# A gated attention and mixture-of-experts kernel: attention and expert 0 in two halves of the tokens, a chain each, and the inverse deviation as GpSimd's power

## The chip, the cores and the metric

One core of a Trainium2 chip. The metric is the device time of one execution in microseconds. TensorE's clock has two levels here, 1.2 and 2.4 GHz, which the profile shows as a granted clock of 0.50 and 1.00.

## The reference, cut to what matters

Sixteen sequences of 56 tokens with 128 features: 896 tokens. First an attention by autocorrelation over the time shifts, with a gate, then a mixture of eight experts, with a gate. Everything is float32.

```python
x = x + tanh(g_xattn) * xattn(layernorm(x), ctx, ctx)
x = x + tanh(g_ffn) * ffn(layernorm(x))

def xattn(query, key, value):                 # 16 heads of 8 features
    Q, K, V = query @ Wq + bq, key @ Wk + bk, value @ Wv + bv     # ctx cut to 56 tokens
    corr = irfft(rfft(Q) * conj(rfft(K)))     # along the tokens
    w, idx = top_k(corr.mean(features), 4)    # of the 56 shifts, for each head
    w = softmax(w)
    out = sum_k w[k] * roll(V, idx[k])
    return out @ Wo + bo

def ffn(x):                                   # 8 experts, 128 -> 512 -> 128
    logits = x @ Wr + br
    weights = softmax(logits, all but the top two masked out)
    h = gelu(x @ W1[e] + b1[e])
    return sum_e (h @ W2[e] + b2[e]) * weights[:, e]
```

## The kernel before, in words

**Layout.** The tokens are 8 tiles of 112 (two sequences each, `NT`, `PT`), in two halves of 4 tiles (`HT`). Half a set of spectra is `HS` = 464 columns, half the tokens `TOK` = 448 columns. The five engines have a queue each, written out by hand, each in the order of the program; they meet at semaphores. PSUM is one tensor `bank` of eight banks, and each step has its bank.

**Attention.** TensorE turns context and normalised input into spectra (L658), projects them to keys, values and queries (`project_spectra`, L664; a bias opens each at L648). ScalarE takes the projected spectra (`take`, L357 to L364); VectorE multiplies queries by keys (L496) and adds the products (L261). TensorE sums per head (L691) and turns back to correlations (L698). VectorE finds the four largest shifts and their weights (L519 to L535), TensorE transposes these (L710) and takes their spectra (L714), VectorE puts them into the columns that own them (`wown`, L543), TensorE repeats them over the rows (L724), VectorE multiplies them with the values (L496) and adds (L261), TensorE makes the output products (L730) and turns them back into tokens (L735) on top of the residual (L718). Each step is done for both halves before the next step begins, on every engine.

**Normalising** (`normalise` of VectorE, L459 to L485): four or eight statistics (L457), eight aggregations (L463), a variance with epsilon (L465), and a guess with two Newton steps for its inverse root, ten dependent small instructions from L465 to L476, each waiting for the one before; then the shift (L478) and the tiles, some by VectorE (L484), some by ScalarE (L354). All eight tiles together, once for the input and once for the attended tokens.

**Fillers.** `keep_busy` (L639) issues products of zeros of 512 columns on TensorE, which nobody reads: 13 at the start, 4 ahead of the transposed weights, 2 ahead of their spectra, 8 ahead of the transposed normalised tokens (L644, L707, L711, L751).

**Experts.** Float32 by three products of a rounded lead and its rest: `weh`, `wel` for the weights, `xth`, `xtl` for the tokens, `hidh`, `hidl` for the hidden values. An expert has four chunks of 128 hidden features; a chunk `n` (0 to 31) is `hidden(n)` (L772, six products of 448 columns: three operand pairs by two halves), ScalarE's Gelu (L409) and lead (L416), VectorE's rest (L617), and `project(n)` (L799, six products). TensorE's order is `hidden(n + 2)`, `project(n)`. Chunks 0 and 31 are split into halves at Gelu, lead and rest. The routing (L568 to L589 on VectorE, a tanh on ScalarE at L431) runs in VectorE's queue behind the rests of chunks 0 and 2; `turn_routes` (L780) stands in TensorE's queue before `project(3)`, and the turned routes go to DRAM and back, spread over the partitions (L283, L290).

**Taking an expert.** VectorE multiplies an expert's sum with its routes into `scaled` (`take_expert`, L604; expert 0 into `acc`), which lies over `kf` and `cf` in the rows; GpSimd adds `scaled` to `acc` (L329), and VectorE may take the next expert only after that, since there is one `scaled` for each half:

```python
if e >= 2:
    ve.wait_ge(acc_ok, 2 * (e - 2) + half + 1)
```

The takes of expert 2 stand behind the rests of chunks 13 and 14 in VectorE's queue (the table `takes`, L610), those of expert 0 behind chunks 7 and 8.

**GpSimd's queue** (L299 to L337): `centre`, the residual with the output bias (`xres`, L308), then for each of the eight experts its weights' rest (`wel`, L323), for experts 2 to 7 the lead too (`weh`, L321; ScalarE does those of experts 0 and 1 at L376), and only behind all eight the additions of L329, for expert 1 with the attended tokens (L333). At the end it does 160 of the last 448 columns (L337). The experts' weights come through a ring of three slots; a load waits until the expert three before is split (L276). SP issues experts 0 to 6, then waits for the routes.

Of the kernel before, what the change touches and what calls it, by code (L numbers as in the profile page):

```python
# [10 lines left out]
I32 = mybir.dt.int32  # L29
# [16 lines left out]
FILL_START, FILL_TOP, FILL_STEP, FILL_NORM = 13, 4, 2, 8  # L46
# [11 lines left out]
GUESS = float(0x5F1FFFF9)  # L58
STEP_A, STEP_B = 0.703952253, 0.703952253 * 2.38924456
# [44 lines left out]
def build(nc, x, tab_ctx, w_attn, bias_rows, gates, shared_rows, cols, w_experts, tab_b, out, route_dram):  # L104
    with ExitStack() as stack:
# [22 lines left out]
        xres = sb("xres", [PT, NT, D])  # L128
        stat = sb("stat", [PT, NT, 6])
        mv = sb("mv", [PT, NT, 2])  # L130
        var = sb("var", [PT, NT])
        rs_a = sb("rs_a", [PT, NT])
        rs_b = sb("rs_b", [PT, NT])
        rs_c = sb("rs_c", [PT, NT])
        rs_d = sb("rs_d", [PT, NT])
# [64 lines left out]
        dve = sem("dve_done")  # L200
        c_spec, cf_ok = sem("context_spectra"), sem("context_spectra_in_sbuf")
        norm_ok, xn_v, xn_s = sem("norm_factors"), sem("xn_by_vector"), sem("xn_by_scalar")
        x_spec, xf_ok = sem("x_spectra"), [sem("x_spectra_in_sbuf0"), sem("x_spectra_in_sbuf1")]
        k_proj, v_proj, q_proj = sem("k_projected"), sem("v_projected"), sem("q_projected")
        k_ok, v_ok = sem("k_in_sbuf"), sem("v_in_sbuf")
        qk_mul, heads, rsb_ok = sem("queries_times_keys"), sem("head_sums"), sem("head_sums_in_sbuf")
        corr, ntop_ok, cexp_ok = sem("correlations"), sem("top_found"), sem("correlation_exponentials")
        wraw_ok, wt_mm, wt_ok = sem("shift_weights"), sem("shift_weights_transposed"), sem("shift_weights_t_in_sbuf")
        ws_mm, wown_ok, warm_ok = sem("weight_spectra"), sem("weight_spectra_in_their_columns"), sem("filler_cleared")
        dc_ok = sem("length_in_row")  # L210
        wrep, of_mul = sem("weight_spectra_repeated"), sem("weights_times_values")
        qk_ok = [sem(f"cross_spectra{half}") for half in range(2)]
        of_ok = [sem(f"output_spectra{half}") for half in range(2)]
        stat_ok = sem("statistics")
# [7 lines left out]
        lead_s, lead_p, we_split, pool = sem("weights_lead_by_scalar"), sem("weights_lead_by_pool"), sem("weights_split"), sem("pool_done")  # L222
# [3 lines left out]
        last_half, sum_v, sum_p = sem("last_expert_half"), sem("sum_complete_by_vector"), sem("sum_complete_by_pool")  # L226
        stored = sem("stored")

        BY_SCALAR = ((3, 6, 7), (3, 6))
        LEAD_BY_SCALAR = 2  # L230

# [6 lines left out]
        CUT = 288  # L238

        def norm_counts(n, times):  # L240

            before = sum(len(tiles) for tiles in BY_SCALAR[:times])
            if n in BY_SCALAR[times]:
                return xn_s, before + BY_SCALAR[times].index(n) + 1
            return xn_v, times * NT - before + [i for i in range(NT) if i not in BY_SCALAR[times]].index(n) + 1

        IN_HALVES = (0, E * HC - 1)

        def parts(n):

            return [(0, slice(0, 1)), (1, slice(1, 2))] if n in IN_HALVES else [(0, slice(0, 2))]

        def upto(n, part=None):

            last = len(parts(n)) if part is None else part + 1
            return n + (1 if n > 0 else 0) + last
# [9 lines left out]
        def _(sp):  # L266
# [3 lines left out]
            sp.dma_start(rows_sb[:, :, :], bias_rows).then_inc(in_rows, 16)  # L270
# [3 lines left out]
            def load_expert(e):  # L274
                if e >= RING:
                    sp.wait_ge(we_split, 2 * (e - RING + 1))  # L276
# [8 lines left out]
            for e in range(E):  # L285
                if e == ROUTES:
                    load_expert(E - 1)
                if e >= ROUTES:
                    sp.wait_ge(scaled_ok, 2 * (e - ROUTES + 1))
                sp.dma_start(route_b[:, e % ROUTES, :, :], route_dram[e:e + 1].broadcast_to([D, 2, TOK])).then_inc(in_route[e], 16)  # L290
            for half in range(2):
                sp.wait_ge(sum_v, half + 1)
                if half == 1:
                    sp.wait_ge(sum_p, 1)
                sp.dma_start(out[:, half, :], o_sb[:, half, :]).then_inc(stored, 16)
# [3 lines left out]
        def _(gp):  # L299
            by_vector = [NT - len(tiles) for tiles in BY_SCALAR]  # L300
            gp.wait_ge(in_tb, 16)
            gp.wait_ge(xn_v, by_vector[0])
            gp.tensor_scalar(centre[:, :], ident, 1.0 / D, None, ALU.subtract).then_inc(centre_ok, 1)
# [4 lines left out]
            gp.tensor_tensor(xres[:, :, :], x_sb[:, :, :], shared[:, 0:D].unsqueeze(1).broadcast_to([PT, NT, D]),  # L308
                             ALU.add).then_inc(xres_ok, 1)

            for e in range(E):
                gp.wait_ge(in_we[e], 16)
                if e == 0:
                    gp.wait_ge(of_ok[0], 1)
                if e == 1:
                    gp.wait_ge(xn_v, sum(by_vector))
                for k in range(2):
                    if e < LEAD_BY_SCALAR:
                        gp.wait_ge(lead_s, 2 * e + k + 1)
                    else:  # L320
                        gp.tensor_copy(weh[:, e, k, :], we_sb[:, e % RING, k, :]).then_inc(lead_p, 1)  # L321
                        gp.wait_ge(lead_p, 2 * (e - LEAD_BY_SCALAR) + k + 1)
# [12 lines left out]
            gp.wait_ge(scaled_ok, 2 * E)  # L335
# [517 lines left out]
```

## Time and profile before

| | us |
|---|---|
| median of 3 runs | 133.5 (132.34 to 134.25) |
| the profiled execution | 132.46 |
| its span, first to last instruction | 130.2 |
| TensorE busy | 117.5 (90%) |
| VectorE busy | 89.9 (69%) |
| ScalarE busy | 80.5 (62%) |
| GpSimd busy | 62.9 (48%) |
| mean granted clock of TensorE | 0.956 |

The profile comes from one execution; its own time is 132.46 us, and the 2.26 us between that and the span lie outside the first and last instruction. "Busy" counts instructions at work, waits excluded; a float32 product on TensorE is several passes, so busy doesn't mean at its peak. L12 is line 12 of the kernel before. PE is TensorE's products, PEld its weight loads, DVE VectorE, ACT ScalarE, POOL GpSimd, SP SyncE.

### The profile page before, as it was taken

To read this page: it belongs to the slowest core of one execution; us is meant where nothing else is said; L and a number is where in the kernel's file an instruction comes from. 1 tells how busy PE (TensorE), PEld (TensorE's weight loads), DVE (VectorE), ACT (ScalarE), POOL (GpSimd) and SP (SyncE) were. 2 spreads that over 40 slices of the span, in tenths; PEclk is the share of its full clock that TensorE was granted. 3 is DMA by queue.
4 is the path that set the end of the run, shared out by engine and by line. 5 is a ranking of instruction groups with operands and counts; after the bars stand their busy time and mean duration, and the time that the engine had idled before them with its cause. 6 is when DMAs were issued, how large, how long until landed. Compare 5 with 4: busy or idle time off the path is not lost.

```text
span 130.2 us, 1685 instructions
## 1 busy us (share of the span) xinstructions
PE 117.5 (90%) x575; PEld 94.7 (73%) x575; DVE 89.9 (69%) x175; ACT 80.5 (62%) x107; POOL 62.9 (48%) x50
## 2 busy tenths in 40 slices
PE   6999969998878993959999999999999999999950
PEld 2397555544465891939999999999999999999930
DVE  1583687529386498999679877775775775775991
ACT  3027764401355755928878878878878878878900
POOL 0001460005203999999999999980330330330802
PEclk9999995559999999999999999999999999999998
DMA  3896000000310215400891340030040030000003
GB/s 93 234 406 249 0 0 5 3 0 0 101 60 0 82 79 161 162 6 9 238 337 43 107 146 0 0 141 0 0 141 3 5 141 0 0 0 0 0 0 141
DMA packets 3833, 10.07 MB, mean 77 GB/s; under 512 B 697, under 2 KB 1066, under 8 KB 3826
## 3 DMA queue, kind: packets, MB, share of 16 engines
q1 hardware_dynamic: 3154, 9.43, 21.5%
q10 hardware_dynamic: 672, 0.55, 1.5%
q8 instruction: 4, 0.07, 0.2%
q14 instruction: 3, 0.02, 0.1%
HBM read 9.49 MB, written 0.49 MB: 77 GB/s over the span
## 4 chain that ended last, share of the span: by engine, by line
PE 70%; DVE 14%; ACT 5%; issue 5%; POOL 2%; POOLq 1%; DVEq 0%
PE bank L772 23%; PE bank L799 22%; PE bank L641 7%; PE bank L658 3%; ACT prod L409 3%; POOL cf L329 2%; DVE hidl L617 2%; PE bank L664 2%; ACT hidh L416 2%; DVE prod L496 2%; DVE tw L496 2%; PE bank L718 2%; PE bank L735 1%; DVE qk L261 1%; PE bank L748 1%
## 5 line engine op out<-in xcount | busy, mean ns | idle before, releaser
L617 DVE TENSOR_TENSOR hidl<-prod,hidh 128x896 fp32r<-128x896 f32 (+1 forms) x34 | 45.3, 1339 | 19.8 <-ACT hidh L416 19.8
L409 ACT ACTIVATE prod<-bank,col_sb 128x896 f32<-128x896 f32 (+1 forms) x34 | 32.9, 967 | 14.5 <-PE bank L772 11.8
L323 POOL TENSOR_TENSOR wel<-we_sb,weh 128x512 fp32r<-128x512 f32 x16 | 25.6, 1604 | 20.9 <-issue 19.9
L416 ACT CAST hidh<-prod 128x896 fp32r<-128x896 f32 (+1 forms) x34 | 30.5, 899 | 1.0
L329 POOL TENSOR_TENSOR cf<-cf,kf 128x448 f32<-128x448 f32 x12 | 17.9, 1496 | 26.6 <-DVE kf L604 26.4
L799 PE MATMUL bank<-hidl,weh 128*128 128x448 f32 x64 | 18.5, 368 | 2.2 <-DVE hidl L617 2.2
L772 PE MATMUL bank<-xth,weh 128*128 128x448 f32 x64 | 18.6, 366 | 0.3 <-ACT xth L404 0.3
L772 PE MATMUL bank<-xtl,weh 128*128 128x448 f32 x64 | 18.6, 367 | 0.0
L772 PE MATMUL bank<-xth,wel 128*128 128x448 f32 x64 | 18.5, 365 | 0.0
L799 PE MATMUL bank<-hidh,weh 128*128 128x448 f32 x64 | 18.4, 367 | 0.0
L799 PE MATMUL bank<-hidh,wel 128*128 128x448 f32 x64 | 18.3, 365 | 0.0
L799 PEld LDWEIGHTS bank<-hidl,weh 128*128 128x128 f32 x64 | 11.9, 188 | 3.8 <-DVE hidl L617 2.8
L772 PEld LDWEIGHTS bank<-xth,weh 128*128 128x128 f32 x64 | 12.0, 188 | 1.4 <-issue 0.5
L772 PEld LDWEIGHTS bank<-xtl,weh 128*128 128x128 f32 x64 | 12.0, 188 | 1.3 <-DVE xtl L562 0.3
L799 PEld LDWEIGHTS bank<-hidh,wel 128*128 128x128 f32 x64 | 12.0, 188 | 1.0
L772 PEld LDWEIGHTS bank<-xth,wel 128*128 128x128 f32 x64 | 12.0, 188 | 0.9
L799 PEld LDWEIGHTS bank<-hidh,weh 128*128 128x128 f32 x64 | 11.9, 188 | 0.9
L321 POOL CAST weh<-we_sb 128x512 fp32r<-128x512 f32 x12 | 12.2, 1017 | 0.0
L641 PE MATMUL bank<-filler 128*128 128x512 bf16 x27 | 10.2, 540 | 1.2 <-DVE filler L451 1.2
L604 DVE SCALAR_TENSOR_TENSOR kf<-bank,col_sb,route_b 128x448 f32<-128x448 f32 x14 | 9.4, 676 | 0.0
L641 PEld LDWEIGHTS bank<-filler 128*128 128x128 bf16 x27 | 3.5, 139 | 5.6 <-issue 3.6
L392 ACT ACTIVATE y_sb<-bank,tanh_g 116x512 f32<-116x512 f32 x2 | 1.4, 690 | 8.6 <-PE bank L730 8.6
(118 smaller groups left out, 116.7 us busy)
## 6 DMA issues: line engine op xcount, KB each, us to landing
we_sb<-in_w_experts SPq DMA_DIRECT2D x8, 512.0 KB, 5.0
route_b<-route_scratch SPq DMA_DIRECT2D x8, 448.0 KB, 3.6
out<-vf SPq DMA_DIRECT2D x2, 224.0 KB, 1.9
tb<-in_tab_b SPq DMA_DIRECT2D x1, 297.0 KB, 6.3
ta_c<-in_tab_ctx SPq DMA_DIRECT2D x1, 274.8 KB, 4.9
wa_sb<-in_w_attn SPq DMA_DIRECT2D x1, 256.0 KB, 5.7
x_sb<-in_x SPq DMA_DIRECT2D x1, 224.0 KB, 3.8
x_sb<-in_x ACTq DMA_DIRECT2D x1, 224.0 KB, 4.1
```

The source lines that it names most:

```text
L321: gp.tensor_copy(weh[:, e, k, :], we_sb[:, e % RING, k, :]).then_inc(lead_p, 1)
L323: gp.tensor_tensor(wel[:, e, k, :], we_sb[:, e % RING, k, :], weh[:, e, k, :].bitcast(F32), ALU.subtract).then_inc(we_split, 1)
L329: gp.tensor_tensor(acc[:, half, :], acc[:, half, :], scaled[:, half, :], ALU.add).then_inc(acc_ok, 1)
L409: act.activation(hid[:, n % 2, halves, :], bank[:, 2 * (n % 2):2 * (n % 2) + 2, 0:TOK][:, halves, :], ACT.Gelu, bias=col_sb[:, P_B1 + n:P_ ...
L416: act.copy(hidh[:, n % SLOTS, halves, :], hid[:, n % 2, halves, :]).then_inc(hid_hi, 1)
L496: return ve.tensor_tensor(products, a.unsqueeze(1).broadcast_to([D, kinds, HS]), pair, ALU.mult).then_inc(multiplied, 1)
L604: ve.scalar_tensor_tensor(out=into[:, half, :], in0=bank[:, 6 - 2 * (e % 2) + half, 0:TOK], scalar=col_sb[:, P_B2 + e:P_B2 + e + 1], in1=r ...
L617: ve.tensor_tensor(hidl[:, n % SLOTS, halves, :], hid[:, n % 2, halves, :], hidh[:, n % SLOTS, halves, :].bitcast(F32), ALU.subtract).then ...
L641: pe.matmul(bank[:, into, :], filler[:, 0:D], filler[:, :], start=True, stop=True)
L658: return pe.matmul(bank[:, first + i // HT, (i % HT) * PS:(i % HT + 1) * PS], src[:, i, :], ta[:, A_FWD:A_FWD + PS], start=(i % HT == 0), ...
L772: mm = pe.matmul(bank[:, 2 * slot + half, 0:TOK], w[:, e, 0, cols_], t[:, half, :], start=(k == 0), stop=(k == 2))
L799: mm = pe.matmul(bank[:, 6 - 2 * (e % 2) + half, 0:TOK], w_of(operands[k][0]), operands[k][1][:, slot, half, :], start=(c == 0 and k == 0) ...
```

## The change

- **Two chains.** Every step of attention becomes a function of one half, and each engine's queue is written anew with the first half ahead. Values of a half are projected between head sums and correlations.
- **Inverse deviation.** The Newton steps go. VectorE makes a half's variances, GpSimd raises them to the power -0.5 (`invert`), VectorE goes on with the shift.
- **Expert 0 in halves.** Chunks 0 to 3 run half by half (`HALF[0]`, `HALF[1]`), the first half's chunks ahead, chunks 4 to 30 on both halves as before, 31 in halves.
- **Fillers.** 7 and 5 at the start; none later.
- **GpSimd.** Its queue starts with the load of the bias rows. The rests of experts 0 and 1 are made in pieces of 128 columns and no longer wait for attention's steps. Behind both inversions of the second normalising it waits for the routes (`route_ok`), and then splits experts 2 to 7. The additions stay behind the splits. The last half's sum is all VectorE's.
- **SP.** Experts 0 to 4 are loaded ahead of the routes, 5 to 7 between the loads of the spread routes.
- **ScalarE.** The tanh of the gates comes first; it copies both halves' x spectra and the turned shift weights, which were VectorE's in part.

```diff
-FILL_START, FILL_TOP, FILL_STEP, FILL_NORM = 13, 4, 2, 8
+FILL_FIRST, FILL_SECOND = 7, 5
...
-        BY_SCALAR = ((3, 6, 7), (3, 6))
+        BY_VECTOR = (2, 3)
         LEAD_BY_SCALAR = 2
+        PIECE = 128
...
-            for e in range(E - 1):
+            for e in range(RING + LEAD_BY_SCALAR):
                 load_expert(e)
             sp.wait_ge(route_sb, 2)
...
+                if e >= 1 and e + RING + LEAD_BY_SCALAR - 1 < E:
+                    load_expert(e + RING + LEAD_BY_SCALAR - 1)
...
         def _(gp):
+            gp.dma_start(rows_sb[:, :, :], bias_rows).then_inc(in_rows, 16)
+            gp.memset(minus_half[:, :], -0.5).then_inc(half_ok, 1)
...
+            def invert(times, half):
+                tiles = slice(half * HT, (half + 1) * HT)
+                gp.wait_ge(var_ok, 2 * times + half + 1)
+                gp.tensor_tensor(rstd[:, tiles], var[:, tiles], minus_half[:, :], ALU.pow).then_inc(rstd_ok, 1)
...
+            for e in range(LEAD_BY_SCALAR):
+                gp.wait_ge(in_we[e], 16)
+                for k in range(2):
+                    gp.wait_ge(lead_s, 2 * e + k + 1)
+                    rest(e, k)
+            invert(1, 0)
+            invert(1, 1)
+            gp.wait_ge(route_ok, 1)
+            for e in range(LEAD_BY_SCALAR, E):
+                gp.wait_ge(in_we[e], 16)
+                for k in range(2):
+                    gp.tensor_copy(weh[:, e, k, :], we_sb[:, e % RING, k, :]).then_inc(lead_p, 1)
...
         @block.vector
...
+            variances(0, 0)
...
+            normalise(x_sb, 0, 0)
+            normalise(x_sb, 0, 1)
+            scores(0)
+            scores(1)
+            head_sums(0)
+            shift_weights(0)
+            head_sums(1)
+            weight_sum(0)
+            own_columns(0)
+            shift_weights(1)
+            weight_sum(1)
+            weighted(0)
+            output_spectra(0)
+            own_columns(1)
+            weighted(1)
+            ve.wait_ge(attn, 1)
+            moments(tiled(bank[0:PT, 0, :]), 0)
+            output_spectra(1)
+            variances(1, 0)
+            normalise(x2, 1, 0)
...
+            rest_of_hidden(1, HALF[1])
+            chosen()
+            rest_of_hidden(2, HALF[1])
+            routes()
+            rest_of_hidden(3, HALF[1])
...
         @block.tensor
...
+            head_sums(0)
+            values(0)
+            correlations(0)
+            head_sums(1)
+            weights_turned(0)
+            correlations(1)
+            weight_spectra(0)
+            values(1)
+            repeated(0)
+            weights_turned(1)
+            add_residual(0)
+            weight_spectra(1)
+            output_products(0)
+            repeated(1)
+            attention(0)
+            add_residual(1)
+            centred_router()
+            output_products(1)
+            attended_turned(0)
+            attention(1)
+            tokens_turned(0)
+            logits(0)
+            attended_turned(1)
+            hidden(0, HALF[0])
+            hidden(1, HALF[0])
+            logits(1)
+            hidden(2, HALF[0])
+            project(0, HALF[0])
+            tokens_turned(1)
+            hidden(3, HALF[0])
+            project(1, HALF[0])
+            hidden(0, HALF[1])
+            project(2, HALF[0])
...
+            hidden(4, BOTH)
+            project(2, HALF[1])
+            turn_routes()
+            hidden(5, BOTH)
+            project(3, HALF[1])
```

## Rows read from the trace of the kernel before

**Rows 1.** The page: TensorE's clock in forty slices of 3.26 us, in tenths.

```profile
PEclk9999995559999999999999999999999999999998
```

**Rows 2.** Stretches: length, busy (instructions) by engine, granted clock, DMA share, GB/s.

```profile
25.00:30.00 5.00, 5.00 (x8) 2.15 (x8) 2.40 (x4) 0.00 (x0) 0.00 (x0) 0.51 0.00 0
...
42.00:58.60 16.60, 12.63 (x63) 10.73 (x64) 13.86 (x28) 10.26 (x15) 16.12 (x15) 1.00 0.29 96
58.60:116.90 58.30, 58.30 (x289) 54.02 (x288) 42.37 (x39) 46.98 (x48) 34.83 (x24) 1.00 0.22 73
```

**Rows 3.** The chain that ended last: start, length, what.

```profile
25.13 1.98 PE bank L718 x2
27.11 1.56 PE bank L724 x2
...
33.58 1.90 PE bank L735 x4
...
42.15 1.05 PE bank L772 x3
...
58.55 1.23 PE bank L799 x6
```

**Rows 4.** Timeline of VectorE and GpSimd in attention: start, length, instruction.

```profile
14.21 1.12 DVE L496 TENSOR_TENSOR prod<-bank,kf 128x928 f32<-128x928 f32 x1 [2.32 <-PE bank L664]
...
14.69 0.61 POOL L306 TENSOR_SCALAR shared<-shared,tanh_g 112x128 f32<-112x128 f32 x1 [3.60 <-ACT tanh_g L373]
...
15.37 0.64 DVE L261 TENSOR_TENSOR qk<-prod 128x464 f32<-128x464 f32 x1
15.39 2.85 POOL L308 TENSOR_TENSOR xres<-x_sb,shared 112x1024 f32<-112x1024 f32 x1
...
34.47 1.92 DVE L457 BATCH_NORM_STATS2 stat<-bank 112x6 f32<-112x128 f32 x8 [2.08 <-PE bank L735]
...
37.17 0.17 DVE L465 TENSOR_SCALAR var<-mv 112x8 f32<-112x8 f32 x1
...
39.20 0.17 DVE L478 SCALAR_TENSOR_TENSOR shift<-mv,rstd 112x8 f32<-112x8 f32 x1
```

**Rows 5.** Stretches of half a microsecond, columns as in rows 2.

```profile
18.00:18.50 0.50, 0.00 (x0) 0.00 (x0) 0.50 (x1) 0.32 (x2) 0.23 (x1) 1.00 0.00 0
...
19.50:20.00 0.50, 0.50 (x11) 0.38 (x10) 0.19 (x1) 0.00 (x0) 0.00 (x0) 0.67 0.00 0
...
30.00:30.50 0.50, 0.50 (x3) 0.14 (x1) 0.50 (x2) 0.00 (x0) 0.00 (x0) 1.00 0.00 0
```

**Rows 6.** Timeline of ScalarE: chunk 0 in halves.

```profile
43.22 1.24 ACT L409 ACTIVATE prod<-bank,col_sb 128x448 f32<-128x448 f32 x2 [0.78 <-PE bank L772]
44.36 1.02 ACT L416 CAST hidh<-prod 128x448 fp32r<-128x448 f32 x2
```

**Rows 7.** Timeline of GpSimd from 43 to 80 us.

```profile
43.52 0.61 POOL L321 CAST weh<-we_sb 128x512 fp32r<-128x512 f32 x1
...
48.72 1.28 POOL L323 TENSOR_TENSOR wel<-we_sb,weh 128x512 fp32r<-128x512 f32 x1
...
57.43 1.61 POOL L321 CAST weh<-we_sb 128x512 fp32r<-128x512 f32 x1
...
76.19 2.01 POOL L329 TENSOR_TENSOR cf<-cf,kf 128x448 f32<-128x448 f32 x1
...
91.57 1.16 POOL L329 TENSOR_TENSOR cf<-cf,kf 128x448 f32<-128x448 f32 x1 [4.14 <-DVE kf L604]
```

**Rows 8.** Timeline of VectorE: the route weights, and the taking of expert 2.

```profile
56.75 0.82 DVE L589 SCALAR_TENSOR_TENSOR route<-lexp,tanh_g,linv 112x64 f32<-112x64 f32 x1
...
80.09 1.09 DVE L617 TENSOR_TENSOR hidl<-prod,hidh 128x896 fp32r<-128x896 f32 x1 [0.94 <-ACT hidh L416]
81.09 0.68 DVE L604 SCALAR_TENSOR_TENSOR kf<-bank,col_sb,route_b 128x448 f32<-128x448 f32 x1
82.51 1.94 DVE L617 TENSOR_TENSOR hidl<-prod,hidh 128x896 fp32r<-128x896 f32 x1 [0.74 <-ACT hidh L416]
```

More of the change, by code:

```diff
@@ L236, in tiled, with normalised, unit, split @@
             return t.rearrange("p (i d) -> p i d", d=D)
[L238 to L256, printed above, removed]
+        def normalised(i, times):
+            half, j = i // HT, i % HT
+            if j < BY_VECTOR[times]:
+                return xn_v, times * 2 * BY_VECTOR[0] + half * BY_VECTOR[times] + j + 1
+            by_scalar = [HT - n for n in BY_VECTOR]
+            return xn_s, times * 2 * by_scalar[0] + half * by_scalar[times] + j - BY_VECTOR[times] + 1
+        def unit(n, half):
+            if n < HC:
+                return n + 1 + HC * half
+            return n + HC + 1 + (half if n == LAST else 0)
+        SPLITS = [2 * (H // PIECE if e < LEAD_BY_SCALAR else 1) for e in range(E)]
+        def split(experts):
+            return sum(SPLITS[:experts])
+        BOTH = slice(0, 2)
+        HALF = (slice(0, 1), slice(1, 2))
         def add_products(engine, products, out_, done):
@@ L433, in _ @@
+            chunk(2, HALF[1])
+            chunk(3, HALF[1])
+            for n in range(HC, LAST):
+                chunk(n, BOTH)
+            chunk(LAST, HALF[0])
+            chunk(LAST, HALF[1])
         @block.vector
@@ L508, in _, with head_sums @@
+            def head_sums(half):
                 ve.wait_ge(heads, half + 1)
@@ L546, in _, with weighted @@
                                         op0=ALU.mult, op1=ALU.mult).then_inc(wown_ok, 1)
-            for half in range(2):
+            def weighted(half):
                 ve.wait_ge(wrep, half + 1)
@@ L693, in _, with correlations @@
                 mm.then_inc(heads, 1)
-            for t in range(2):
+            def correlations(t):
                 pe.wait_ge(rsb_ok, t + 1)
@@ L732, in _, with attention @@
                 mm.then_inc(y_mm, 1)
-            for half in range(2):
+            def attention(half):
                 pe.wait_ge(y_ok, half + 1)
@@ L761, in hidden, with tokens_turned @@
+            def tokens_turned(half):
+                pe.wait_ge(wrc_ok, 1)
+                for i in range(half * HT, (half + 1) * HT):
+                    pe.wait_ge(*normalised(i, 1))
+                    mm = pe.transpose(bank[:, 6 + half, (i % HT) * PT:(i % HT + 1) * PT], xn[:, i, :], ident[0:PT, 0:PT])
+                mm.then_inc(xt_mm, 1)
+            def hidden(n, halves):
+                e, c, slot, last = n // HC, n % HC, n % 2, halves.stop - 1
                 if c == 0:
-                    pe.wait_ge(we_split, 2 * e + 1)
+                    pe.wait_ge(we_split, split(e) + SPLITS[e] // 2)
```

563 lines of the change are left out of this document (280 added, 283 removed).

## The prediction

> **What bounds the kernel now.** I read the totals and the forty slices of the page first. TensorE is busy 117.5 of 130.2 us, and its clock line stands at 5 tenths in the seventh to ninth slice [rows 1]. Next the stretches: from 58.6 to 116.9 TensorE is busy all 58.30 us at the full level (2.4 GHz), with VectorE at 42.37 and ScalarE at 46.98. Between 42.0 and 58.6 it works 12.63 of 16.6 us. Between 25 and 30 it is busy throughout, but at a granted clock of 0.51 (1.2 GHz) [rows 2]. So 24 chunks of an expert (twelve products each) take 58.3 us, 2.43 each, and all 32 need 77.8 us. The change can't shorten that; it can only start it earlier and lose less in it. The chain of waits gives the marks of today: the shift weights' spectra are repeated over the rows from 27.11 to 28.67, the second attention product ends at 35.48, the first expert product starts at 42.15, and chunk 3, the last of expert 0, ends at 58.55+1.23=59.8 [rows 3].
>
> **1. Scores to repeated weights.** Before the scores little changes: the statistics still run beside the context spectra, and the Newton steps taken out there save nothing as long as GpSimd's power needs under about 1 us. Following the queues I have half 0 normalised at 8.4, its spectra taken at 10.4, its queries projected at 12.1 and its keys taken at 12.95. Its product (1.12) and sum (0.64) then begin at 13.0 instead of 14.21 [rows 4]. One half now needs: product and sum 1.8, head sums and correlations 1.6, shift weights 1.2 (both halves take 1.9 now), turn and spectrum 0.9, own columns 0.65. In between stand, on VectorE, the second half's scores (to 17.1) and, on TensorE, the first half's values and later the second's. I get correlations(0) at 17.9, shift weights(0) at 19.2, own columns at 21.3, values(1) done at 22.7, repetition(0) from 22.75 to 24.3: 4.35 us earlier than now, with TensorE at the low level as it is now.
>
> **2. The clock.** TensorE stands still from 18.0 to 18.5 at 1.00; in 19.5 to 20.0 the granted clock is 0.67, a mixture of the two levels, and half of full speed behind it. It is back at 1.00 in 30.0 to 30.5 [rows 5], after the five busy microseconds of [rows 2]. The change keeps the narrow products and the waits of that place, takes six fillers away and puts two value products of 464 columns between. I take fall and rise where they are now. Then residual(0) 1.98 [rows 3], weight spectrum(1) 0.5, output products(0) 1.3 and repetition(1) 1.56 end at 30.1, attention(0) at full level at 31.0 (two take 1.90 [rows 3]), and VectorE, which weights the second half until 31.3, ends the first statistics (half of 1.92 [rows 4]) at 32.3. If the level never fell, each of the low products would take half and this would be near 28.5.
>
> **3. Attention to the first expert product.** Behind those statistics come the output sum 0.64, aggregation and variance 0.55, the power, the shift 0.2, three tiles at 0.27; TensorE then does attention(1), turned tokens and logits, ScalarE the lead of 0.49. The power isn't in this trace. GpSimd's nearest rows run from 0.61 us for 128 columns to 2.85 for 1024 [rows 4]; for four numbers a partition I take 0.5, nearest to the short one; below lies at most 0.4 more, since something must be handed over. With the handing over it replaces nine of the ten steps from 37.17 to 39.20 [rows 4], 1.8 us, by 0.7. The eight fillers of 1.7 us ahead of the turned tokens go as well. The first product comes 5.4 us behind statistics(0), at 37.7 instead of 42.15: 4.5 earlier (33.9, or 8.2 earlier, if the level stays up).
>
> **4. Expert 0 in halves.** A half chunk costs TensorE 1.21 and ScalarE 0.62+0.51=1.13 [rows 6]; ScalarE has 1.3 us more for a tile, the second half's lead and a tanh. Following both queues I find no gap over 0.7 us: eight half chunks 9.7, chunks 4 and 5 hidden 2.4, logits(1) and the second turn 1.3, the turned routes 0.9, gaps 0.8, so 15.1 us to the end of chunk 3 against 17.6 now (59.8-42.15). Chunk 3 ends at 52.8 instead of 59.8: **7.0 us** earlier. SP's new order costs nothing: expert 5 is asked for when expert 2 is split, two experts of GpSimd's pace ahead of its own turn, and the later ones likewise.
>
> **5. What the wait for the routes costs.** Here the gain goes. GpSimd splits experts 2 to 7, twelve pairs of a cast and a difference. Only behind them in its queue stands the first addition, and that frees the one buffer into which VectorE takes expert 2. Now the pairs begin at 43.52 and the addition runs from 76.19 to 78.20 [rows 7]; VectorE asks at 81.09 [rows 8], with 2.9 us to spare. Changed, they begin with the route weights. From those to VectorE's request are 23.5 us now (57.57 to 81.09 [rows 8]) and by the order of chunks 24.0 then. How many pairs fit? One alone is 0.61+1.28=1.9; the six from 57.43 to 76.19 [rows 7], beside this same VectorE work, took 18.76, 3.1 each, the later ones 2.8. So 6+5.2/2.8=7.9 pairs are done. The 4.1 that are left go at 1.9, since VectorE stands still, 7.8 us, and the addition takes 1.16: VectorE waits **9.0 us** in chunk 13. The bounds: at 2.3 (the six pairs from 43.52 to 57.43) 10.4 pairs are done and the wait is 4.2; at 3.1 throughout it is 9.2.
> The Trainium skill's "GPSIMD Engine Reference", section 1 (Specifications), says that GpSimd contends with VectorE instructions that have two SBUF inputs. If these excluded it wholly, ten of them at 1.09 would leave 13.1 us, 6.9 pairs and a wait of 10.9. The rows agree in direction (1.09 against 1.94 for the same instruction [rows 8]) and show less than exclusion, so the sum goes by them.
> TensorE has work in hand: the rest of chunk 14 would end 1.8 us behind the request, and isn't due before 86.1 on today's times, so 3.2 us are absorbed. TensorE stands for 5.8, and 0.2 more a chunk later. After so long a stand it may come back at the low level. The price is half the time until it rises; the low stretch of now is 10.3 us (19.7 to 30.0), dense work should end it sooner. I take 1.5, with 0 and 5 as ends. Together 7.5.
>
> **6. The end.** The last sum is VectorE's alone, 0.63 instead of 0.46 beside GpSimd's 0.79, which decides now: -0.2.
>
> **Sum.** -7.0+7.5-0.2=+0.3 on this execution's 132.46 us (span 130.2 and 2.26 around it): 132.8. The median of the three runs, 133.5, lies 1.0 above it. I state 132.5.
>
> **Rivals.**
> *A, the forecast*: the gain is made and GpSimd's late start takes it back. 132.5; own range 129.5 to 135.5. For it speak the queue's order and [rows 7].
> *B, less is taken back*: pairs at 2.3, a wait of 4.2, TensorE stands 1.2 with the end of it, no low level: 132.46-7.0+1.2-0.2=126.5; if the level stays up in attention too, 3.7 less: 122.8. For it: GpSimd's rate before 57 us; against it: the rate after.
> *C, slower*: TensorE is at the low level when the experts start, since eight fillers went and only narrow products and waits lie between statistics(0) and the first one. Half chunks cost 2.4 instead of 1.2 until it rises; ten such microseconds lose 5: 132.5+5=137.5. It decides at the first expert product, 0.4 us each instead of 0.2. Against it: the clock line is at 9 in every slice from 30 us on [rows 1], gaps included.
> *D, slower*: the power is long. At 2.85 us the first costs 1.8 (1 us has cover) and that of half 0 behind attention 2.3: 136.6. The point is a power above 1.5 us.
> The same "GPSIMD Engine Reference", section 2.1 (Instruction dispatch), states some 6 us of loading at the first call of a freshly loaded function. Paid once at the start, 5 of it without cover, it would give 137.5. No row here shows one.
>
> **Chances.** A 0.42, B 0.31, C 0.17, D 0.10. Two per cent, about what a measurement of this kernel can tell from no change, are 130.8 and 136.2. Faster: nearly all of B and a fifth of A, 0.38. Slower: most of C, half of D, a little of A, 0.20. Same 0.42. The range 126 to 137 leaves out the low part of B and the high one of C.
>
> **What would show it.** Right: first expert product near 37.7; chunk 3 ending near 53; GpSimd's first cast at the route weights; VectorE's take of expert 2 waiting some 9 us for GpSimd's addition, and a hole of 6 us in TensorE in chunks 14 to 16. Wrong: pairs near 2 us and no hole (B); granted clock 0.5 inside expert 0 (C); power rows over 1.5 us (D). If the clock is 1.00 from 19.5 to 30, step 2 was wrong and 3.7 us more come off.

## The result, and the profile after

The changed kernel takes 135.24 us (median of 20 runs, 133.15 to 137.0) against 133.61 for the kernel before (20 runs, 130.57 to 134.89), with a ratio of 1.019 and a 95% interval of 1.013 to 1.026. Every ratio here compares the means of those executions alone that lie within 1.5% of the fastest of their kernel (9 of the 20 against 5 of the 20; the quotient of the two medians is 1.012), and the profiles of no_route_wait, before_with_route_wait and before_wait_additions come from executions above that, so that only their stretches and waits are read. So the changed kernel is slower, by 1.9% by the ratio. The forecast was 132.5 us in a range of 126 to 137, so the time lies in the range, but on the other side of the kernel before than the forecast did. The profiled execution took 134.32 us with a span of 132.5.

First the page, as in [rows 1]: TensorE's busy time and granted clock in slices of 3.31 us.

```profile
PE   6399997999789999999999990199999999999960
...
PEclk9977998569999999999999999658999999999998
```

Three things are new. TensorE is idle for most of the second slice and its clock drops in the third and fourth, before the scores of attention. The low stretch of attention is shorter. And in the middle of the experts stands a hole of two slices, with low clock in it and behind it. The same in stretches, with the columns of [rows 2]:

```profile
42.00:58.60 16.60, 16.60 (x89) 15.00 (x88) 12.70 (x31) 14.70 (x23) 7.91 (x6) 1.00 0.21 61
58.60:116.90 58.30, 52.31 (x246) 47.53 (x245) 37.20 (x33) 39.50 (x41) 38.29 (x31) 0.94 0.22 74
...
79.70:85.70 6.00, 0.04 (x1) 0.00 (x0) 2.48 (x2) 0.00 (x0) 5.34 (x6) 0.82 0.00 1
85.70:90.40 4.70, 4.67 (x13) 4.17 (x14) 3.62 (x3) 3.19 (x4) 4.48 (x4) 0.50 0.26 98
```

From 42.0 to 58.6, where TensorE worked 12.63 us before [rows 2], it works all 16.60. From 58.6 to 116.9, where it never paused, it now loses 6.0 us, and in 79.7 to 85.7 only GpSimd and, at the end, VectorE work. The marks that answer to [rows 3], from the timeline of TensorE: first expert product, last product of chunk 3, last products ahead of the hole (the time in which TensorE stands still), first behind it.

```profile
38.80 0.45 PE L839 MATMUL bank<-xth,weh 128*128 128x448 f32 x1
...
53.03 0.37 PE L864 MATMUL bank<-hidl,weh 128*128 128x448 f32 x1
...
79.17 0.57 PE L864 MATMUL bank<-hidh,wel 128*128 128x448 f32 x2
85.73 1.12 PE L864 MATMUL bank<-hidl,weh 128*128 128x448 f32 x2 [5.99 <-DVE hidl L583]
```

The first expert product is at 38.80 instead of 42.15 and chunk 3 is over at 53.4 instead of 59.8, 6.4 us ahead. Then TensorE waits 5.99 us for the rest of a hidden chunk, and that is VectorE's. VectorE's timeline says why it is late, and GpSimd's says what it waits for; they answer to [rows 8] and [rows 7].

```profile
50.10 0.28 DVE L616 SCALAR_TENSOR_TENSOR route<-lexp,tanh_g,linv 112x64 f32<-112x64 f32 x1
...
73.69 1.43 DVE L583 TENSOR_TENSOR hidl<-prod,hidh 128x896 fp32r<-128x896 f32 x1 [1.23 <-ACT hidh L410]
83.19 0.68 DVE L627 SCALAR_TENSOR_TENSOR kf<-bank,col_sb,route_b 128x448 f32<-128x448 f32 x1 [8.07 <-POOL cf L326]
83.79 1.88 DVE L583 TENSOR_TENSOR hidl<-prod,hidh 128x896 fp32r<-128x896 f32 x1
```

```profile
50.45 0.93 POOL L318 CAST weh<-we_sb 128x512 fp32r<-128x512 f32 x1 [10.99 <-DVE route L616]
...
80.76 1.26 POOL L320 TENSOR_TENSOR wel<-we_sb,weh 128x512 fp32r<-128x512 f32 x1
81.98 1.12 POOL L326 TENSOR_TENSOR cf<-cf,kf 128x448 f32<-128x448 f32 x1
```

Behind the rest of chunk 13 (ready at 75.1) VectorE is to take expert 2; it starts at 83.19, after 8.07 us, released by GpSimd's addition of 81.98. That addition stands behind twelve pairs of cast and difference, and the first of these has itself waited 10.99 us for the route weights. The chain of waits goes through GpSimd's pairs from 50.45 to 82 without a gap; on the page GpSimd has 26% of the chain that ended last, against 2% before.

### The profile page after: what moved, and what is told of

Read it like the earlier page. It is cut to its first block, busy times and chain, and to the rows that moved or that the text cites. A ratio compares the mean times of both kernels' runs of the same rounds, so it can differ in the third digit from the quotient of the medians.

```text
span 132.5 us, 1688 instructions
## 1 busy us (share of the span) xinstructions
PE 116.3 (88%) x560; PEld 95.6 (72%) x560; DVE 82.8 (62%) x163; ACT 82.9 (63%) x117; POOL 65.7 (50%) x68
## 4 chain that ended last, share of the span: by engine, by line
PE 48%; POOL 26%; ACT 9%; DVE 7%; DMA 4%; issue 3%; DVEq 0%; POOLq 0%
PE bank L864 17%; PE bank L839 15%; POOL wel L320 14%; POOL weh L318 9%; DMA rows_sb<-in_bias_rows 4%; PE bank L710 3%; ACT prod L402 3%; PE bank L731 2%; ACT hidh L410 2%; PE bank L773 2%; PE bank L787 2%; POOL cf L326 1%; PE bank L706 1%; PE bank L780 1%; PE bank L702 1%
## 5 line engine op out<-in xcount | busy, mean ns | idle before, releaser
L583 DVE TENSOR_TENSOR hidl<-prod,hidh 128x896 fp32r<-128x896 f32 (+1 forms) x37 | 46.3, 1257 | 18.2 <-ACT hidh L410 18.2
L326 POOL TENSOR_TENSOR cf<-cf,kf 128x448 f32<-128x448 f32 x12 | 16.9, 1415 | 24.6 <-DVE kf L627 24.5
L864 PE MATMUL bank<-hidl,weh 128*128 128x448 f32 x64 | 19.8, 378 | 6.0 <-DVE hidl L583 6.0
L839 PE MATMUL bank<-xth,weh 128*128 128x448 f32 x64 | 19.8, 378 | 0.0
L864 PE MATMUL bank<-hidh,weh 128*128 128x448 f32 x64 | 19.5, 374 | 0.0
L864 PE MATMUL bank<-hidh,wel 128*128 128x448 f32 x64 | 19.4, 373 | 0.0
L320 POOL TENSOR_TENSOR wel<-we_sb,weh 128x512 fp32r<-128x512 f32 x12 | 18.4, 1532 | 1.0
L282 POOL TENSOR_TENSOR rstd<-var,minus_half 112x4 f32<-112x4 f32 x4 | 4.2, 1047 | 15.3 <-DVE var L496 15.3
L287 POOL TENSOR_TENSOR wel<-we_sb,weh 128x128 fp32r<-128x128 f32 x16 | 7.1, 476 | 6.4 <-ACT weh L370 6.4
L513 DVE TENSOR_TENSOR prod<-bank,kf 128x928 f32<-128x928 f32 x2 | 2.2, 1124 | 6.8 <-ACT kf L365 6.8
```

The source lines that it names most:

```text
L282: gp.tensor_tensor(rstd[:, tiles], var[:, tiles], minus_half[:, :], ALU.pow).then_inc(rstd_ok, 1)
L287: gp.tensor_tensor(wel[:, e, k, at:at + PIECE], we_sb[:, e % RING, k, at:at + PIECE], weh[:, e, k, at:at + PIECE].bitcast(F32), ALU.subtra ...
L320: gp.tensor_tensor(wel[:, e, k, :], we_sb[:, e % RING, k, :], weh[:, e, k, :].bitcast(F32), ALU.subtract).then_inc(we_split, 1)
L326: gp.tensor_tensor(acc[:, half, :], acc[:, half, :], scaled[:, half, :], ALU.add).then_inc(acc_ok, 1)
L583: ve.tensor_tensor(hidl[:, n % SLOTS, halves, :], hid[:, n % 2, halves, :], hidh[:, n % SLOTS, halves, :].bitcast(F32), ALU.subtract).then ...
L839: mm = pe.matmul(bank[:, 2 * slot + half, 0:TOK], w[:, e, 0, cols_], t[:, half, :], start=(k == 0), stop=(k == 2))
```

## The experiments

**1. Without GpSimd's wait for the routes** (no_route_wait).

```diff
-            gp.wait_ge(route_ok, 1)
             for e in range(LEAD_BY_SCALAR, E):
```

> The changed kernel with one wait less: GpSimd no longer waits for the route weights before it splits experts 2 to 7. Theory 'late start': the splits begin at 39.5 instead of 50.45, right behind the last power, and end some 10 us earlier, near 72; VectorE's 8.1 us wait in chunk 13 and TensorE's hole of 6.0 us go, and with them the 4.7 us at the low level and the slower steps behind it. The routing chain and the halves' rests run beside GpSimd again and lose up to 1.5. Time 135.2-9+1=127 (ratio to before 0.95). Rival 'pace': the splits are slowed by the contention as much as they gain by the start, or the hole has another cause; then it stays within 2 us of 135 (ratio near 1.01).

Measured: 133.85 us, ratio 1.005 (0.998 to 1.011). The expectation missed by 7 us: the hole went to under 2 us (waits of 1.14 and 0.56), but the time hardly moved. Two things took its place. In the routing stage TensorE lost what it had gained, from the profile of this kernel:

```profile
42.00:52.00 10.00, 6.94 (x38) 5.51 (x37) 9.90 (x21) 6.57 (x13) 9.68 (x9) 1.00 0.00 1
```

where the changed kernel works 10.00 of the same 10 us. VectorE is busy 9.90 of them, and TensorE's longest wait there (2.31 us) is for it: it has become the bound. From the first expert product to the end of chunk 3 it takes 19.7 us instead of 14.6. And GpSimd, now early, stood still:

```profile
67.88 0.61 POOL L317 CAST weh<-we_sb 128x512 fp32r<-128x512 f32 x1 [12.88 <-DMA we_sb<-in_w_experts]
...
84.34 1.16 POOL L325 TENSOR_TENSOR cf<-cf,kf 128x448 f32<-128x448 f32 x1
```

It waited 12.88 us for expert 5, whose load stands in SP's queue behind the trip of the routes (asked for at 61.88), so its first addition was at 84.34, no earlier than with the wait. With the wait in place that order of the loads had cost nothing.

**2. The same with the loads of experts 5 and 6 ahead** (no_wait_loads_ahead): SP's loop runs to expert 6 before it waits for the routes, and takes 7 where the kernel before does.

> The changed kernel without the wait for the routes and with SP's loads of experts 5 and 6 ahead of the routes as in the kernel before: GpSimd was idle for 12.9 us waiting for expert 5 when only the wait went. Theory: splits done near 70, no wait at expert 2; what is left against the additions-between version is the routing stage beside GpSimd, 3 to 4 us in TensorE between 42 and 58. 126+3.5=129.5 (ratio 0.97). Rival 'the routing stage is not slowed by GpSimd': 126.

Measured: 134.16 us, ratio 0.997 (0.992 to 1.002). No hole is left behind 58 us (the last wait of TensorE in its timeline is that for the routes at 57.73), and still the kernel is 8 us slower than with the wait and the additions between (experiment 4), where I expected 3.5. The difference lies in one stage: from the first expert product to the end of chunk 3 it takes 21.6 us here and 14.6 in experiment 4, and from there to the last product 65.7 in both. In that stage VectorE's rests and its routing chain run beside GpSimd, and the route weights come at 57.7 instead of 50.4. Single rows show it. VectorE's second logit step is L592 here and L593 in the changed kernel, an addition of 64 columns with two inputs in SBUF; first this kernel's rows, GpSimd's and VectorE's, then the changed kernel's, where GpSimd stands still.

```profile
42.19 1.68 POOL L319 TENSOR_TENSOR wel<-we_sb,weh 128x512 fp32r<-128x512 f32 x1
...
42.90 1.06 DVE L592 TENSOR_TENSOR logit<-logit,shared 112x64 f32<-112x64 f32 x1
```

```profile
41.74 0.23 DVE L593 TENSOR_TENSOR logit<-logit,shared 112x64 f32<-112x64 f32 x1
```

VectorE's step ends at 43.96 and GpSimd's subtraction at 43.87; the step behind it (L596, 1.18 us) ends at 45.85 and GpSimd's next subtraction at 45.77. In these rows a short VectorE instruction lasts until GpSimd's long one is over. The wait for the routes is therefore worth about 7 us in the two-chain kernel (span 130.6 here, 123.4 in experiment 4), and 5 in the stage of experiment 1, where GpSimd soon stood still. It is what makes the routing stage fast. Experiments 2 and 4 also differ in the order of SP's loads; that these don't matter to the stage isn't tested apart.

**3. The first addition ahead of the last splits** (first_addition_ahead). The wait stays; GpSimd adds expert 1 behind the split of expert 5.

```diff
+                if e == 5:
+                    add_expert(1)
```

> The changed kernel with the wait for the routes kept, but GpSimd's two additions of expert 1 (and of the attended tokens) placed ahead of the splits of experts 6 and 7 instead of behind them. Theory 'late start': it is the place in GpSimd's queue that costs, so the addition comes at 73.6, about when VectorE asks (75.1); at most 1 us of wait is left, no hole, the level stays up: 135.2-9=126.5 (ratio 0.945), a little better than without the wait, since the routing chain stays undisturbed. If instead experts 6 and 7 become late at TensorE, a hole comes at chunks 24 and 28: they are needed at 104 and 114 and split by 90, so I expect none. Rival 'something else in chunk 13': 135, the hole stays.

Measured: 132.65 us, ratio 0.994 (0.989 to 1.000). The wait in chunk 13 went, and came back one expert later, since the addition of expert 2 was still behind the splits of 6 and 7, from this kernel's timeline:

```profile
93.40 0.68 DVE L633 SCALAR_TENSOR_TENSOR kf<-bank,col_sb,route_b 128x448 f32<-128x448 f32 x1 [6.86 <-POOL cf L319]
...
95.40 0.67 PE L870 MATMUL bank<-hidl,weh 128*128 128x448 f32 x2 [3.95 <-DVE hidl L589]
```

A hole of 3.95 us instead of 5.99, with low clock behind it again. The mechanism holds, my edit was one addition short. Another part of the miss isn't the hole's: in this profiled execution, as in that of experiment 1, the first expert product comes at 40.8 and 40.7 instead of 38.8, though up to there both kernels are the changed one. Five fillers behind the bias rows took 2.31 us in both instead of 1.58, and the context spectra began at 10.5 and 10.6 instead of 9.05. So kernels that are alike up to there start up to 2 us apart in different executions, and a mark of one profile carries that with it. GpSimd's whole list has to be laid against the times at which each addition is asked for, not only the first.

**4. All additions between the splits** (additions_between): experts 1 and 2 are added behind the split of 5, expert 3 behind that of 6.

```diff
+                for done in {5: (1, 2), 6: (3,)}.get(e, ()):
+                    add_expert(done)
```

> The changed kernel, wait for the routes kept, with GpSimd's additions set between the splits: those of experts 1 and 2 behind the split of expert 5, that of 3 behind the split of 6, the rest at the end. With only the first one ahead the hole came back at expert 3, one addition later. Theory 'the additions' place in GpSimd's queue': no wait over 1.5 us on VectorE in chunks 13 to 26, no hole over 1 us in TensorE, clock 1.00 from 30 us on, steps of 2.43 throughout: 9 us less than the changed kernel, 126 (ratio 0.945). Rival 'GpSimd has too little time in any order': the wait turns up at expert 3 or 4, or experts 6 and 7 come late; over 130.

Measured: 126.09 us, ratio 0.934 (0.925 to 0.943). The time is as expected to a tenth of a microsecond; the ratio is below the expected 0.945, since the kernel before, measured beside it, had 134.44. The same take of expert 2, from its timeline, waits for nothing that is listed, and GpSimd's first addition, the second row, is done before it, at 74.7:

```profile
75.58 0.67 DVE L633 SCALAR_TENSOR_TENSOR kf<-bank,col_sb,route_b 128x448 f32<-128x448 f32 x1
```

```profile
73.56 1.15 POOL L319 TENSOR_TENSOR cf<-cf,kf 128x448 f32<-128x448 f32 x1
```

From 39 us on TensorE has no wait over 0.3 us, and its clock is 1.00 from 34 to 123 us. The order of eight instructions in GpSimd's queue (the additions of three experts and of the attended tokens, two halves each) decides 9 us, by the medians (135.24 and 126.09) as by the spans (132.5 and 123.4).

**5. The wait for the routes in the kernel before** (before_with_route_wait), with SP's loads as the change has them.

```diff
+                if e == LEAD_BY_SCALAR:
+                    gp.wait_ge(route_ok, 1)
...
-            for e in range(E - 1):
+            for e in range(RING + LEAD_BY_SCALAR):
```

> The kernel before with this one part of the change: GpSimd waits for the route weights before expert 2, and SP loads experts 5 to 7 between the spread routes (without that the routes would wait for the splits). Theory 'late start': splits from 57.6, 7.7 pairs done when VectorE asks at 81.1, a wait of 9, a hole in TensorE of 6, 2 at the low level, under 1 gained by an undisturbed routing: 133.6+7.5=141 (ratio 1.055). Rival 'the halves cost it': under 2 us of difference, ratio 1.00 to 1.015.

Measured: 137.25 us, ratio 1.022 (1.006 to 1.037). The hole is there without any halves or chains, and it is larger: VectorE waits 9.98 us, TensorE 7.29.

```profile
87.76 0.68 DVE L606 SCALAR_TENSOR_TENSOR kf<-bank,col_sb,route_b 128x448 f32<-128x448 f32 x1 [9.98 <-POOL cf L331]
...
89.95 1.11 PE L801 MATMUL bank<-hidl,weh 128*128 128x448 f32 x2 [7.29 <-DVE hidl L619]
```

The time is smaller than expected because the gain was mis-sized: not under 1 but some 3.6 us, TensorE being busy 16.27 us from 42.0 to 58.6 instead of 12.63.

**6. The kernel before with the wait and the additions between** (before_wait_additions).

> The kernel before, whole steps and all, with only GpSimd's and SP's part mended: the wait for the routes, SP's loads between, the additions of experts 1 to 3 between the splits. It isolates what the wait is worth in the kernel before, and by difference what the two chains are worth. With the wait alone the route weights came at 53.8 instead of 57.6 and TensorE was busy 16.3 of 16.6 us between 42.0 and 58.6 (12.6 before): 3.7 us less, and no hole: 134-3.7=130.3 (ratio 0.972). The chains and halves are then worth 126.1-130.3, 4 us. Rival 'the wait and the order do it all': 127 or less.

Measured: 128.78 us, ratio 0.972 (0.956 to 0.988), the ratio expected. So GpSimd's and SP's lists alone make the old kernel 2.8% faster (1.2 to 4.4%). What the two chains with halves, fillers and power are worth beside that is less certain. The ratios 0.972 and 0.934, each against its own runs of the kernel before, give 5 us; rows_by_sp of experiment 9, which differs from experiment 4 in one load and was measured together with this kernel, has 0.960, which gives 1.6; and chunk 3 ends at 56.2 in this profile and at 53.3 in that of experiment 4, 2.9 us apart. So it is some 2 to 5 us, less than the order of the additions.

**7. Fillers until the bias rows are there** (fillers_to_the_rows), in the changed kernel.

```diff
-FILL_FIRST, FILL_SECOND = 7, 5
+FILL_FIRST, FILL_SECOND = 13, 0
```

> The changed kernel with 13 fillers at the start and none behind the opened projections (7 and 5 before): TensorE works until 6.7, when the bias rows land, and keeps the level, so the context spectra take 2.0 us instead of 3.9 and start at 7.8 instead of 9.05. Theory 'late bias rows and low level': scores(0) begin near 13.2 instead of 15.7, all behind that moves up by 2 to 2.5; the hole in chunk 13 moves with it but keeps its size. 135.2-2.3=133 (ratio 0.995). Rival 'the start is hidden elsewhere' (keys or normalising set scores(0)): under 0.7 us.

Measured: 131.76 us, ratio 0.994 (0.983 to 1.004), against 1.019: 3.4 us less where 2.3 were expected, 2.9 by the spans (129.6 and 132.5). First the rows of the changed kernel, then those of this one: opened projections and context spectra on TensorE, the first scores on VectorE.

```profile
6.71 1.03 PE L706 MATMUL bank<-dc,rows_sb 1*128 1x8 f32 x8 [2.37 <-DMA rows_sb<-in_bias_rows]
9.05 3.29 PE L710 MATMUL bank<-ta_c 112*128 112x116 f32 x16
...
15.68 1.12 DVE L513 TENSOR_TENSOR prod<-bank,kf 128x928 f32<-128x928 f32 x1 [6.46 <-ACT kf L365]
```

```profile
6.93 1.02 PE L706 MATMUL bank<-dc,rows_sb 1*128 1x8 f32 x8 [0.32 <-DMA rows_sb<-in_bias_rows]
7.88 2.04 PE L710 MATMUL bank<-ta_c 112*128 112x116 f32 x16
...
13.27 1.12 DVE L513 TENSOR_TENSOR prod<-bank,kf 128x928 f32<-128x928 f32 x1 [3.83 <-ACT kf L365]
```

The rows are used at nearly the same time, 6.71 and 6.93, but here TensorE works until then, waits 0.32 us instead of 2.37 and stays at the full level (a granted clock of 0.99 or more from 3 to 19 us): the spectra take 2.04 instead of 3.29 us and start 1.2 earlier, so the scores start 2.4 us earlier. The hole behind is 6.00 us, as large as before: the route weights move with everything else, so the start makes no difference to it.

**8. Both together** (additions_and_fillers).

> The same with 13 fillers ahead of the bias rows and none behind. If both effects are independent they add: 126-2.3=123.7 (ratio 0.927). If the earlier start only makes GpSimd late again (its splits begin with the routes, so they move along), under 1 us is left of the 2.3.

Measured: 122.65 us, ratio 0.915 (0.908 to 0.922). The two effects add: the fillers give 2.6 us by the ratios of experiments 4 and 8 (2.1 by the spans), where 2.3 were expected.

**9. Who loads the bias rows** (rows_by_sp; rows_by_sp_fillers): experiments 4 and 8 with the load in SP's queue.

> The changed kernel with the additions between and the bias rows loaded by SP, third in its queue as in the kernel before, with 7 and 5 fillers. If it is GpSimd's queue that makes the rows late (5.35 us from issue to landing), they land by 5.5, TensorE's idle stretch from 4.35 is 1.1 us instead of 2.4, and the clock stays at 1.00: 126.1-2=124 (ratio 0.925). Rival 'small loads land late on any queue while the large ones run' (the gates took 5.3 and the columns 6.1 on ScalarE's queue): they land at 6.5 to 7 and nothing changes, 126.

> The same with 13 fillers ahead of the rows and none behind. If the rows land by 5.5 the fillers, which end at 6.6, cover them and give 122.6 or 0.3 less than with GpSimd's load; if they land as late as before, 122.6 as well. It tells whether the load's queue matters once the clock is held (I expect it doesn't: within 0.7 us of 122.65).

Measured: 126.5 us (ratio 0.960, 0.947 to 0.973; the kernel before, measured beside it, was low at 132.14) and 122.31 us (0.933, 0.923 to 0.942). The first was expected at 124 if GpSimd's queue were the cause, and it came as its rival said. In rows_by_sp the rows land at 6.4 instead of 6.6 and TensorE still waits:

```profile
6.49 1.02 PE L712 MATMUL bank<-dc,rows_sb 1*128 1x8 f32 x8 [2.15 <-DMA rows_sb<-in_bias_rows]
```

So it isn't GpSimd's queue that makes 1.5 KB late: they land about as late on SP's. That the large loads under way are the cause isn't tested. The filled kernels are alike at 122.65 and 122.31, and either is the fastest of all. That rows_by_sp and experiment 4 are alike in time (126.5 and 126.09) but have ratios of 0.960 and 0.934 shows how far the kernel before moves from one set of runs to the next, 132.14 and 134.44: ratios of different sets carry that 2%.

**10. Newton steps in place of the power** (newton), in the changed kernel, a half at a time.

> The changed kernel with the Newton steps of the kernel before on VectorE, for a half at a time, in place of GpSimd's power. A half costs nine more links, 1.8 us, in place of the power's 1.05 and 0.25 of handing over: 0.5 us later on half 0 behind attention, and VectorE is held while it was free for other work, at most 1 more for half 1. 135.2+0.7=136 (ratio 1.023). Rival 'the power is what made the first part fast': over 2 us slower.

Measured: 138.89 us, ratio 1.034 (1.025 to 1.044): 1.5% or 2 us slower than the changed kernel by the ratios, 3.7 by the medians and 4.1 by the spans, in any case more than the 0.7 expected. The spans divide like this. The first expert product came at 40.68 instead of 38.80, 1.9 us later; from there to the end of chunk 3 it took 17.6 us instead of 14.6; behind that it was 0.8 faster. The first part can't be put down to the steps: no_route_wait and first_addition_ahead, which have the power, start their first expert product at 40.7 and 40.8. At the start two steps of the second half's chain were caught beside GpSimd's residual (two instructions from 10.02 to 12.51):

```profile
9.94 0.16 DVE L505 TENSOR_TENSOR rs_b<-rs_c 112x4 f32<-112x4 f32 x1
10.14 1.17 DVE L506 TENSOR_TENSOR rs_b<-rs_b,var 112x4 f32<-112x4 f32 x1
11.34 1.19 DVE L507 TENSOR_SCALAR rs_d<-rs_b 112x4 f32<-112x4 f32 x1
```

Four columns take 1.17 us instead of 0.16, and even half 0's shift, which stands behind that chain in VectorE's queue, waited for it until 12.90. But TensorE was at the context spectra until 14.0 in this execution, so nothing shows that this cost time. The 3.0 us of expert 0 are the steps': the second half's chain (39.98 to 41.93) stands in VectorE's queue ahead of the rest of the first half's tokens, TensorE waits for that rest inside chunk 0, and behind the wait its clock falls to the low level for 3.4 us. The wait of 1.19 and half of the 3.4 make 2.9 of the 3.0. This is the mark of rival C, the low level inside expert 0, in a kernel where the wait brings it.

```profile
40.68 0.45 PE L853 MATMUL bank<-xth,weh 128*128 128x448 f32 x1
...
42.52 0.47 PE L853 MATMUL bank<-xtl,weh 128*128 128x448 f32 x1 [1.19 <-DVE xtl L589]
...
44.40:47.80 3.40, 3.40 (x12) 2.99 (x12) 2.42 (x14) 2.17 (x5) 0.00 (x0) 0.53 0.00 0
```

The last line is a stretch, with the columns of [rows 2]. The power is right, and not for its own length: a power of 112x4 is 1.03 us (four of them 1.01 to 1.11), five times a Newton link, but it replaces nine links and leaves VectorE free.

## Why the prediction was right and wrong

**Step 5, the late splits: the mechanism right, its price too small, and this is the term that failed.** The sum took the hole and what follows it at 7.5 us. From the end of chunk 3 to the last product it takes 74.7 us (53.40 to 128.14) against 65.7 before, so the price was 9.0. VectorE's wait was to be 9.0 and was 8.07; 7.9 pairs were to be done at its request and 8.6 were. TensorE's work in hand was to absorb 3.2 us and absorbed 2.1. These two errors offset each other, so that the hole, to be 5.8 and 0.2 a chunk later, was 5.99 with nothing a chunk later: close in part by luck. The low level behind it was to cost 1.5. The stretch of 4.7 us at 0.50 holds five pairs of products of 0.75 us in place of 0.41 and a first one of 0.9, so it cost 2.2. Experiments 3 to 5 show the mechanism: moving the additions takes the hole away, moving one of them moves it by one expert, and the wait alone brings it into the kernel before.

**What was not in step 5.** Behind the hole all products ran at 0.413 us a pair instead of 0.405 nearly to the end: the interval from 90.80 to 95.75, two chunks, is 4.95 us, and 4.86 would be two of 2.43. Over fifteen chunks that is 0.7 us, a term the prediction didn't have. With 5.99 and 2.2 it makes 8.9 of the 9.0. It isn't the hole's own price, though. Experiment 7 (fillers_to_the_rows) has a hole of 6.00 us too, and behind it two chunks take 4.86, from its timeline:

```profile
98.22 0.57 PE L839 MATMUL bank<-xth,weh 128*128 128x448 f32 x2
...
103.08 0.56 PE L839 MATMUL bank<-xth,weh 128*128 128x448 f32 x2
```

There the price of the hole is 74.1-65.7=8.4 us.

**Steps 1 to 3: the sum 1.1 us short, from two errors of opposite sign.** The first scores were to begin at 13.0 and began at 15.68. The premise that failed is "before the scores little changes": I took the new place of the bias rows' load and the 7 fillers as free. The fillers run out at 4.35, the rows land at 6.6, TensorE resumes at 6.71 at the full level, falls to the low one at about 8.5, and the context spectra take 3.3 us, which I had at 2.0. Experiment 7 shows this term as 2.4 us at the scores. Against that the low stretch of attention came at 22.2 instead of 19.7 and ended at 28.8 instead of 30.0: 6.6 us where I had 10.3. The sum of it: attention(0) begins at 31.16 where I had 30.1, and the first product comes at 38.80 where I had 37.7. Step 3 itself held: from the first statistics to the first product it takes 5.6 us, where I had 5.4, though the power, 0.5 in my sum, was 1.04 there (1.01 to 1.11 in its four calls), and from variance to shift it took 1.15 instead of 0.7. I had named the uncertainty of the low stretch (3.7 us for a level that stays up), but the direction in which it went was luck.

**Step 4: right, and for a reason I didn't name.** Chunk 3 ended 14.6 us behind the first product, where 15.1 were forecast; at 53.4, where 52.8 were. The step found "no gap over 0.7 us", and nowhere says that this holds only because GpSimd stands still beside the routing chain. Experiments 2 and 5 show that this is worth 3.5 us in the kernel before (chunk 3 ends at 56.3 instead of 59.8) and 7 in the changed one. So the change's wait for the routes was itself the largest gain and, through the queue behind it, the largest loss.

**The sum, and the time stated.** The profile is 2.3 us longer (132.5 against 130.2), where my sum had -7.0+7.5-0.2=+0.3. Measured, the same terms are -6.4+9.0-0.3: 1.5 of the 2.0 between are step 5's price, 0.6 are the first marks. The sum is a small difference of two large terms, so errors of a fifth and less in them decide its sign. A second fault came on top. The sum was positive for the profiled execution, and that lay 1.0 under the median; carried over to the median, +0.3 is 133.8, not 132.5, and even on the profiled execution it is 132.8. The prediction gives no reason for going down to 132.5. So it turned its own sum, hardly any loss, into a small gain; 133.8 would have had the direction right and the size still short by 1.4.

**The rivals.** B (less taken back) didn't come: pairs took 2.9 us each beside VectorE. C (experts started at the low level) didn't: the clock is 1.00 from 35.5 to 42, without the eight fillers, and first products take 0.20, so those fillers weren't needed here. D (a long power) didn't either: its mark was a power above 1.5 us, and 1.01 to 1.11 were measured, twice what the sum had. The first power took 1.03 us like the others, 0.16 behind the variance that it waited for, so no loading is seen in this case. By the Trainium skill's "GPSIMD Engine Reference", section 2.1 (Instruction dispatch), the first call of a freshly loaded function would have had some 6 us. The rows of experiment 2 show VectorE's step with two inputs in SBUF at 1.06 us beside GpSimd and at 0.23 without. The same page of the Trainium skill, section 1 (Specifications), names this contention, and the trace agrees in direction; it gives no size there.

**What stays open.** Why products run 2% slower for a while at a granted clock of 1.00. It is so from 90.8 us on in the changed kernel, behind the hole of before_with_route_wait, and from 48.0 to about 57 us in newton; it isn't so behind the holes of fillers_to_the_rows (6.00 us), newton (5.61) and first_addition_ahead (3.95). So the length of the hole doesn't decide it, and no run tells a cause. Why the start differs by 2 us between executions of the same instructions stays open too. Whether 13 fillers are the best number wasn't tried.

## What to carry to other kernels

A wait that is added to keep an engine quiet delays everything in its queue, and the instruction that matters may be the last: write down for each later instruction when its consumer asks for it, and put those that free a buffer between the bulk work. Here that order was worth 9 us, more than the whole restructuring; a hole also costs its echo at the low clock, here 2 us for 6. And sum against the time that you will be compared with: a sum of +0.3 on an execution below the median is no forecast of a gain. Where the sum is a difference of two large terms, its sign is worth no more than the worse of them.

## What the runs showed of the hardware that was not expected

- VectorE instructions of 4 and 64 columns with two inputs in SBUF took 1.06 to 1.18 us beside a long GpSimd instruction, and 0.16 to 0.23 without. They ended within 0.1 us of GpSimd's. The one-input step of newton at 11.34 (1.19 us) did the same. An instruction of 64 columns with one input in PSUM (no_wait_loads_ahead, at 42.65) took 0.21 while GpSimd's subtraction of 42.19 was running. The loss is per instruction, so a chain of small ones loses most.
- GpSimd's power of 112x4 took 1.01 to 1.11 us in all four calls, while its cast of 128x512 takes 0.61 and its addition of 128x448 takes 1.12 at the shortest. No run varies the columns of the power.
- A load of 1.5 KB took 5.35 us on GpSimd's queue and 4.7 on SP's (rows_by_sp), while the DMA engines were at 0.8 of their time and more.
- After an idle stretch of 2.4 us at the start (4.35 to 6.71) the clock was at 0.50 from 8.5 on, although TensorE had been at work again for 1.8 us by then. In no_route_wait and newton the record shows 1.00 there, and yet the five fillers took 2.31 us, as at 0.50 in first_addition_ahead: the lengths of the rows tell more than the clock beside them.
